# Six banks in place of four for the last heads' scores, with the router's transposes and two layer tiles in the same ring

## What is computed

```
x = x + 0.5 * ffn(layernorm(x))
x = x + attention(layernorm(x))        # 16 heads of 32, causal, latent width 64
x = x + 0.5 * ffn(layernorm(x))

ffn:  scores = x . w_router; the 768 highest of the 1024 tokens become gelu(x @ w_block),
      the others pass as they are
attention: Q = x Wq^T; latents k, v = x Wk^T, x Wv^T (64 wide)
      logits = (Q q_to_latent) k^T / sqrt(64), causal, softmax
      heads = (softmax v) v_up; out = heads Wout^T
```

## Time and profile before

| | before |
|---|---|
| median of three runs | 2492.73 us (2490.47 to 2492.91) |
| the profiled execution | 2491.35 us, its span 2489.6 us |
| granted clock, mean | 0.963 |
| TensorE busy | 2253.0 us (90%) |
| VectorE busy | 1807.2 us (73%) |
| ScalarE busy | 1181.1 us (47%) |
| GpSimd busy | 395.8 us (16%) |

### The profile page before, as it was taken

One profiled execution on the slowest core, in us unless ns is written; L12 is line 12 of the kernel. 1 busy time (PEld: TensorE's weight loads), 2 busy tenths in 40 slices (PEclk: granted clock), 3 DMA queues, 4 the chain that ended last, 5 costly groups with the idle time before them and its releaser, 6 DMA issues.

```text
span 2489.6 us, 53117 instructions
## 1 busy us (share of the span) xinstructions
PE 2253.0 (90%) x21504; PEld 1395.5 (56%) x21504; DVE 1807.2 (73%) x5077; ACT 1181.1 (47%) x2070; POOL 395.8 (16%) x510
## 2 busy tenths in 40 slices
PE   5779999999998999999999999989998899988976
PEld 4534477445674556644566446754476445764445
DVE  5668757887678766787667876778757787678726
ACT  3335543465434654446434464345643455434542
POOL 0101211112101121011111102111111112111121
PEclk9879999899999999999999999989999999999988
DMA  3200021100301002010021101120021100301000
GB/s 131 102 1 3 2 84 53 69 2 6 98 35 69 3 19 85 35 69 3 20 83 52 53 2 53 52 74 29 2 78 59 69 3 2 95 8 69 2 2 34
DMA packets 69601, 106.42 MB, mean 43 GB/s; under 512 B 2544, under 2 KB 32752, under 8 KB 67312
## 3 DMA queue, kind: packets, MB, share of 16 engines
q1 hardware_dynamic: 69360, 103.03, 12.2%
HBM read 64.75 MB, written 37.75 MB: 41 GB/s over the span
## 4 chain that ended last, share of the span: by engine, by line
PE 71%; DVE 15%; issue 6%; ACT 6%; POOL 2%; DMA 0%; DVEq 0%; POOLq 0%; ACTq 0%
PE psum L726 27%; PE psum L739 18%; PE psum L839 9%; PE psum L846 7%; DVE psum L984 4%; PE psum L742 4%; ACT pr L706 4%; DVE part L982 3%; PE psum L768 2%; PE psum L753 2%; DVE junk L932 1%; DVE junk L934 1%; DVE nt_l L907 1%; POOL x L604 1%; ACT nt_h L625 1%
## 5 line engine op out<-in xcount | busy, mean ns | idle before, releaser
L706 ACT ACTIVATE pr<-psum 128x512 f32<-128x512 f32 x1152 | 617.7, 596 | 607.3 <-PE psum L742 607.2
L739 PE MATMUL psum<-qk,qk 32*128 32x512 f32 (+3 forms) x4608 | 519.3, 373 | 95.5 <-DVE part L984 41.7
L984 DVE CUSTOM_DVE_ANT_0 psum<-psum,mask_b 128x512 f32<-128x512 f32 (+3 forms) x1024 | 472.4, 521 | 115.9 <-PE psum L753 114.2
L739 PEld LDWEIGHTS psum<-qk,qk 32*128 32x128 f32 x4608 | 326.4, 190 | 403.6 <-DVE part L984 124.2
L753 PE MATMUL psum<-qk,qk 32*128 32x512 f32 (+3 forms) x4608 | 520.5, 376 | 25.5 <-DVE part L982 19.7
L982 DVE TENSOR_REDUCE part<-psum 128x1 f32<-128x512 f32 x512 | 324.8, 680 | 45.9 <-PE psum L753 43.8
L753 PEld LDWEIGHTS psum<-qk,qk 32*128 32x128 f32 x4608 | 318.5, 191 | 50.1 <-DVE part L982 26.1
L839 PE MATMUL psum<-pr,v_sb 128*32 128x512 f32 (+3 forms) x3072 | 316.6, 508 | 1.6 <-ACT ht L625 1.6
L617 POOL TENSOR_SCALAR_AFFINE_SELECT pr<-pr 128x512 f32<-128x512 f32 x256 | 159.2, 641 | 962.2 <-ACT pr L706 962.2
L846 PE MATMUL psum<-pr,ones 128*32 128x512 f32 (+3 forms) x3072 | 312.0, 501 | 0.0
L646 ACT ACTIVATE norm<-x,nmr,rstd 128x512 f32<-128x512 f32 x192 | 152.4, 811 | 173.0 <-DVE nmr L901 173.0
(11 more groups left out here) (109 smaller groups left out, 3277.6 us busy)
## 6 DMA issues: line engine op xcount, KB each, us to landing
x<-x_dram SPq DMA_DIRECT2D x16, 1024.0 KB, 6.7
spill_x<-x SPq DMA_DIRECT2D x16, 1024.0 KB, 4.7
x<-spill_x SPq DMA_DIRECT2D x16, 1024.0 KB, 7.3
out_dram<-x SPq DMA_DIRECT2D x16, 1024.0 KB, 5.0
w_h<-scratch_o SPq DMA_DIRECT2D x28, 256.0 KB, 3.1
w_l<-scratch_o SPq DMA_DIRECT2D x28, 256.0 KB, 3.3
w_h<-scratch_q SPq DMA_DIRECT2D x6, 1024.0 KB, 4.9
w_l<-scratch_q SPq DMA_DIRECT2D x6, 1024.0 KB, 7.1
```

The source lines that it names most:

```text
L706: nc.scalar.activation(pr_of(b, g, u)[:, 2 * p + place, :], bank(e, place), ACT.Exp, scale=SCALE).then_inc(exp_ready, 1)
L739: eng.matmul(o, (k_h, k_h, k_l)[t][own, P * j:P * (j + 1)], (q_h, q_l, q_h)[t][own, queries], start=(t == 0 and at == 0), stop=False, skip ...
L984: m = nc.vector.tensor_tensor_reduce(scores, scores, mask_b[:, BANK - w:BANK], 1.0, FAR, ALU.add, ALU.max, top_of)
```

## The change

In the last group the pairs of `S` take their four banks from ring A, six banks, as the pairs of `S` and `MX` do. `SC` and `F` 0 and 1 of batches 1 to 7, which had the two banks of ring F, take one bank at a time from ring A too, so that ring F is gone. Pairs of `MX` in group 0 keep ring N. The order of the list, the instructions and their sizes stay as they are.

```diff
         if k in ("S", "MX"):
             early = k == "MX" and e[2] == 0 and e[3] not in (5, 6)
-            own = take("H", 0, 8, 4) if early else take("N", 0, 4, 4) if k == beside[e][0] else take("A", 0, 6, 4)
+            own = take("H", 0, 8, 4) if early else take("N", 0, 4, 4) if k == beside[e][0] == "MX" else take("A", 0, 6, 4)
             banks[e], banks[beside[e]] = own[1::2], own[0::2]
         elif k == "XT":
             own = banks[e] = take("N", 0, 4, 1) if e[2] == 0 else take("A", 0, 6, 1)
         elif k in ("PV", "DEN"):
             own = banks[e] = [6 + (k == "DEN")]
-        elif k == "T" and e[1] == 0 and e[2] > 0:
+        elif (k in ("T", "SC") or k == "F" and e[3] < 2) and e[1] == 0 and e[2] > 0:
             own = banks[e] = take("A", 0, 6, 1)
-        elif (k == "SC" or k == "F" and e[3] < 2) and e[1] == 0 and e[2] > 0:
-            own = banks[e] = take("F", 4, 2, 1)
```

## The result

| | before | after |
|---|---|---|
| median | 2492.01 us (4 runs, 2490.47 to 2492.91) | 2465.3 us (4 runs, 2463.96 to 2468.5) |
| span of the profiled execution | 2489.6 us | 2463.5 us |
| granted clock, mean | 0.963 | 0.963 |
| TensorE busy | 2253.0 us (90%) | 2246.8 us (91%) |

The ratio is 0.9894, with a 95% interval of 0.988 to 0.9909: faster by 1.1%. The forecast was 2468 us.

A forecast was written before the change was run, and what follows sets the result against it. TensorE was taken as nearly the bound in the last groups, held by ScalarE's fourth exp. Terms 15.7 + 4.2 + 2.9 + 0.8 - 0.3 = 23.3 us, off 2491.35, gave 2468.0 us; range 2461 to 2478.

The forecast's parts named there:

- The units: Last groups: pairs wait for the third exp, not the fourth, so 35 waits go; 15.7 us less.
- Unit 0: Start of each last group: only the third maximum and third exp are needed, not the last; 4.2 us less.
- Unit 1: Last groups of batches 0, 1, 3, 4, 6: no more wait for VectorE's copy from XT's bank; 2.9 us less.
- SC: SC in the six-bank ring: TensorE arrives sooner and may wait 0 to 0.1 us for scores; 0.3 us lost in all.
- F 2: Layer tile's wait for F 0's gelu leaves batches 0, 3, 6 and comes to 2, 5; net 0.8 us less.
- Nothing taken back: Behind the last group: TensorE's inputs are ready and later work moves along, so the gain is not given back.
- Rival B: Router chain or gelus behind the group take the gain back; 2487 us, chance 0.04.
- A: In the units the third exp comes just too late, so waits only shrink, half of 15.7 us; 2476 us, chance 0.12.
- C: Granted clock falls inside the last groups and makes it slower; 2512 us with 11 us low in each, chance 0.03.
- D: Clock falls at the output projection hit other batches; 3 to 5 us either way, only widening the range.
- That groups differ by phase: Each batch starts at the same ring phase; group lengths differ by a few tenths between phases; zero, plus or minus 1.

The follow-up runs named there:

- dealing exps 3 and 4 to the shared banks: Changed kernel, with the last group's deal giving the next pair the banks of exps 3 and 4 instead of 1 and 3; 2480.47 us, ratio 0.995.
- The experiment with XT: Changed kernel, with the transpose of the maxima after unit 0 put in the bank unit 1 takes next, batches 0 to 6; 2468.78 us, ratio 0.9901.
- exps 1 and 2: Changed kernel, with the last group's deal giving the next pair the banks of exps 1 and 2; 2472.06 us, ratio 0.9914.
- the other deal in groups 0 to 2: Changed kernel, with scores given a pair's first two banks in groups 0 to 2, so the next pair takes both exps' banks; 2540.52 us, ratio 1.0204.
- the layer tiles from bank 1: Changed kernel, with the ring of layer tiles 2 to 7 set to start at bank 1 in each batch; 2461.25 us, ratio 0.9883.
- the fixed ring of eight: Changed kernel, with the ring of all eight banks set to the same bank at the start of each batch's latents; 2448.39 us, ratio 0.9834.

## Why the prediction was right, and where it was not

The forecast was 2468.0 us, and the median is 2465.3.

- **The units: right.** 15.7 us forecast; the stages give 15.3 - 2.9 = 12.4 in batches 0 to 6, without unit 1, and 3.1 in batch 7, so 15.5; dealing exps 3 and 4 to the shared banks took 15.6 back. That the gain goes with the exp that is waited for, and not with the number of banks, was argued in the prediction and is now shown.
- **Unit 0: right.** 4.2 us forecast, 4.2 measured up to unit 0; the idle time itself fell from 6.9 us over eight batches to 2.6. It ends with the third maximum.
- **Unit 1: right.** 2.9 us forecast. Of the 15.3 us in the last groups 2.9 are unit 1's (32.3 us from unit 0 to unit 1 over seven batches, now 29.4). The experiment with XT shows that the copy can hold unit 1 and for how long.
- **SC: no loss.** 0.3 us was set down; there is no wait. The column of scores was ready at 583.39 and TensorE came at 583.58. Counted from the last maximum, the scores were ready after 10.07 us (10.33 before) and TensorE was there after 10.26, so the margin that was put at nothing was 0.2 us.
- **F 2: right.** 0.8 us forecast, 0.9 measured, and in the batches that were named: the wait left batches 0, 3 and 6 and came to 2 and 5.
- **Nothing taken back: right.** The first tile behind the group is taken at 608.15 with the same 2.74 us of VectorE's wait as before. Rival B is refuted, A by exps 1 and 2, and C by the clock of 1.00 in the groups, both with four banks and waits of 0.38 us and with six and none. The Trainium skill, "TensorE: Matmul & The Clock Gate", section "A second HAM failure mode: psum-queue depth-cycling", tells of a kernel that cycles through the PSUM banks and whose small idles between groups of matmuls come often enough to make the clock swing between its two levels. The traces of these two kernels showed nothing of it in the last groups; the trace of the other deal in groups 0 to 2, with more and longer small waits, is in line with it (last section).
- **The difference of 2.6 us.** It is the part of the 26.1 us that lies in untouched stages. D named it as something that only widens the range. The output projection had three falls of the clock before and one after, 1.6 us each, which are the 3.2 us there; groups 0 went the other way by 2.1 us, with 81.9 us at the low level in batches 1 to 7 before and 85.3 after. Batch 7's end gained 2.3, of which 1.7 stand between unit 8 and the output projection: the clock fell there behind the 1.6 us wait for ScalarE, in the profile before and in that of the layer tiles from bank 1, and in no other of the nine that have this wait. All of it is luck of one execution as far as the runs can say, since the changed kernel alone spreads over 10 us. The second set of runs, 2490.13 and 2464.9 us, has the two kernels 25.2 us apart, where the first has them 26.7.

That groups differ by phase was counted as zero, plus or minus 1. In groups 1 and 2 the clock is 1.00 in both traces, and they bear it out: groups 1 took 0.3 us more in all, and groups 2, without the 4.3 us of idle time at unit 0, 0.1 more. In groups 0 it can't be told from the clock and stays open.

## What to carry to other kernels

When a ring is smaller than two uses of it, a new use waits for the last reader of those banks that it shares with the use before: look up which readers those are, and deal the banks so that they are the early ones. Here it was worth 16 us in the last of the four groups, and the wrong deal in the other three cost 75. Where a ring's uses per round are no multiple of its size, its phase turns with the rounds, and waits that show in some rounds only (batches 1, 2, 3, 5 and 6 here) are a sign of it; setting the ring to a good phase at each round saved 10 us and more. Judge terms of 2 us by their stage and their wait in the trace, since the total of the same kernel moved by 10.

## What was not expected of the hardware

**At the output projection** the granted clock fell only after TensorE had stood idle for long, and then not always. In the ten profiles without the fixed ring of eight, the time from the start of the last product of the values V to the projection's first is 0.55 us in batches 0 and 4, with no idle time in it, 1.85 in batch 3, 2.5 in 2 and 6, and 3.05 in 1 and 5 (1.2, 1.9 and 2.4 us of it idle). The first two tiles behind took 5.7 us in all 30 cases of 0.55 and 1.85 us, and 7.2 to 8.5 us, with the clock at 1.2 GHz for a part, in 22 of the 40 cases of 2.5 us and more. With the time at 0.55 in all batches (two profiles, 14 cases, ten of them in batches that wait otherwise) it fell in none. Which of the 40 fall differs between executions of the same kernel: in batch 6 it fell in the second profile of the changed kernel and not in the first. One fall costs some 1.6 us, and several are at stake, so that they are part of the total's scatter. The two kernels without them have runs 5 us apart, where the changed kernel's are 10; that the falls in groups 0, which remain, make up these 5 was not tested.

**In the groups** a long idle time was not needed. Eleven profiles have a clock of 1.00 in all groups 1 and 2 and all last groups. The twelfth is the other deal in groups 0 to 2, with 16 waits in each group 1, none over 0.81 us, of together 5.3 us, where the changed kernel has 5 waits and 1.1 us in most. It has the clock fall at the start of four groups 2 (batches 1, 2, 6 and 7) and of two last groups (1 and 4). Its batch 1, groups 2 and 3, then the last groups of batches 2 and 4, the granted clock again third from the right:

```profile
542.70:593.80 51.10, 47.68 (x566) 24.62 (x566) 35.76 (x102) 30.66 (x54) 4.94 (x9) 0.93 0.01 2
593.80:628.60 34.80, 34.80 (x405) 16.49 (x406) 25.62 (x81) 19.07 (x37) 9.01 (x14) 0.90 0.01 2
902.70:934.40 31.70, 31.69 (x405) 15.75 (x405) 25.46 (x81) 19.06 (x37) 9.02 (x14) 1.00 0.01 3
1508.20:1541.50 33.30, 33.30 (x405) 16.32 (x405) 25.57 (x81) 19.05 (x37) 9.00 (x14) 0.95 0.01 2
```

TensorE at the start of the second of these: two waits, 2.7 us apart, and the clock falls with the end of the second. The same two stand ahead of all six falls, and ahead of ten starts of such groups without one.

```profile
591.05 0.44 PE L741 MATMUL psum<-qk,qk 32*128 32x384 f32 x2 [0.70 <-ACT pr L708]
...
593.78 1.22 PE L741 MATMUL psum<-qk,qk 32*128 32x512 f32 x8 [0.81 <-ACT pr L708]
```

A last group that waits for nothing took 34.8 us with the fall and 31.7 without. A single wait of 1.09 us, at unit 0 in the kernel before, left the clock at 1.00. That the number of small waits makes the difference is a reading of one profile and not shown.
